# Expert loop: the bias add one slot ahead on GpSimd, the slot's first-layer weights by a DMA, and the relus first on VectorE

## The reference

```
logits = xf @ Wg.T
idx = jnp.argmax(logits, axis=-1)
out = jnp.zeros_like(xf)
for e in range(E):                      # E = 8, D = 128, DF = 512
    m = (idx == e)[:, None].astype(xf.dtype)
    h = jax.nn.relu(xf @ W1[e] + b1[e])
    out = out + m * (h @ W2[e] + b2[e])
...
z = _layer_norm(y + _moe(y, Wg, W1, b1, W2, b2), g2, be2)
```

## Time and profile before

| what | us |
|---|---|
| median of 3 runs | 1211.57 (1209.97 to 1211.81) |
| the profiled execution | 1201.12 |
| its span in the trace | 1199.3 |
| GpSimd busy in the span | 824.3 (69%) |
| VectorE busy | 923.1 (77%) |
| TensorE matmuls busy | 943.2 (79%) |
| ScalarE busy | 592.9 (49%) |
| the expert loop, from 972 to the end | 227 |

### The profile page before, as it was taken

One profiled execution on the slowest core, in us unless ns is written; L12 is line 12 of the kernel. 1 busy time (PEld: TensorE's weight loads), 2 busy tenths in 40 slices (PEclk: granted clock), 3 DMA queues, 4 the chain that ended last, 5 costly groups with the idle time before them and its releaser, 6 DMA issues. The chain is left out here.

```text
span 1199.3 us, 25297 instructions
## 1 busy us (share of the span) xinstructions
PE 943.2 (79%) x5489; PEld 681.6 (57%) x5489; DVE 923.1 (77%) x2728; ACT 592.9 (49%) x1554; POOL 824.3 (69%) x728
## 2 busy tenths in 40 slices
PE   3799999999688688889888816888768578777774
PEld 3465555555366355555555514566567577666663
DVE  3599999999769588888889845766655957777775
ACT  1655545554299466776666525666265013333331
POOL 0388888888422299999999946788144047888885
PEclk9899999999889799999999956999755559999998
DMA  7410000000000400000000051334322022233330
GB/s 213 134 52 1 0 0 0 0 0 1 1 1 1 140 10 9 17 17 9 17 17 18 10 157 40 95 98 105 92 84 79 1 68 83 88 91 91 90 89 24
DMA packets 67117, 61.25 MB, mean 51 GB/s; under 512 B 7812, under 2 KB 54096, under 8 KB 67042
## 3 DMA queue, kind: packets, MB, share of 16 engines
q1 hardware_dynamic: 58978, 41.47, 12.4%
q0 software_dynamic: 6912, 18.36, 5.3%
q10 hardware_dynamic: 1152, 0.52, 0.2%
HBM read 30.97 MB, written 21.50 MB: 44 GB/s over the span
## 5 line engine op out<-in xcount | busy, mean ns | idle before, releaser
L462 PE MATMUL a_pS<-a_kv,utri 128*128 128x360 f32 (+3 forms) x768 | 264.8, 481 | 19.3 <-issue 6.5
L453 POOL TENSOR_TENSOR a_kv<-a_qk,a_vv 128x1152 f32<-128x1152 f32 (+1 forms) x128 | 264.0, 2063 | 13.2 <-DVE a_qk L427 13.2
L558 POOL TENSOR_TENSOR a_tt<-a_tt 128x576 f32<-128x576 f32 (+1 forms) x128 | 156.9, 1226 | 64.4 <-DVE a_tt L542 64.3
L462 PEld LDWEIGHTS a_pS<-a_kv,utri 128*128 128x128 f32 x768 | 136.3, 191 | 100.4 <-DVE a_tt L542 30.5
L542 DVE TENSOR_TENSOR a_tt<-a_pS,a_qk 128x360 f32<-128x360 f32 (+3 forms) x384 | 180.9, 526 | 15.4 <-PE a_pS L462 8.5
L1759 POOL DMA_INDIRECT x_yl<-ys,e_row x72 | 70.1, 974 | 69.5 <-POOLq L1472 54.2
L570 DVE TENSOR_REDUCE a_nd<-a_tt 128x144 f32<-128x720 f32 (+3 forms) x128 | 104.3, 815 | 0.0
L508 ACT ACTIVATE a_tt<-a_pI 128x144 f32<-128x144 f32 (+1 forms) x96 | 40.0, 417 | 111.7 <-PE a_pI L470 111.6
L1765 POOL DMA_INDIRECT out_dram<-x_o,e_row_z x72 | 73.3, 1017 | 25.2 <-DVE x_o L1753 20.8
L1687 ACT ACTIVATE x_hT<-x_pA,x_w 128x128 f32<-128x128 f32 x144 | 45.0, 363 | 89.8 <-PE x_pB L1679 81.9
L501 PEld LDWEIGHTS a_pO<-wgate,a_yT 128*128 128x128 f32 x256 | 42.8, 194 | 81.0 <-issue 50.8
(11 more groups left out here) (260 smaller groups left out, 2437.6 us busy)
## 6 DMA issues: line engine op xcount, KB each, us to landing
ys<-gw SPq DMA_DIRECT2D x16, 256.0 KB, 3.7
xs<-X SPq DMA_DIRECT2D x16, 256.0 KB, 2.3
X<-xs SPq DMA_DIRECT2D x16, 256.0 KB, 5.5
m_kx<-m_kc SPq DMA_DIRECT2D x64, 64.0 KB, 2.0
ys<-X SPq DMA_DIRECT2D x16, 256.0 KB, 3.1
m_ax<-m_pc SPq DMA_DIRECT2D x64, 64.0 KB, 2.0
ys<-U SPq DMA_DIRECT2D x16, 256.0 KB
w<-in_L_ffn_W_dram SPq DMA_DIRECT2D x1, 2048.0 KB
```

The costliest lines, as they stand in the source:

```text
L453: pool.tensor_tensor(kv[:, t % 2, :, :, :], kk.unsqueeze(2).to_broadcast([P, H, J, D]), vv[:, t, :, :].unsqueeze(3).to_broadcast([P, H, J, ...
L462: pe.matmul(pS[c][:, 0:(h1 - h0) * SC], K.utri[:, :], flat[:, h0 * SC:h1 * SC], start=True, stop=True).then_inc(u_done, 1)
L558: pool.tensor_tensor(tt[:, t % 2, :, :, D // 2:D], tt[:, t % 2, :, :, D // 2:D], tt[:, t % 2, :, :, 0:D // 2], ALU.add).then_inc(half_done, 1)
```

## The change

- VectorE no longer copies `w1`. SP's queue issues a DMA of the same 644 numbers by 128 partitions (322 KB) from `K.w1` to the ring instead, SBUF to SBUF, with the expert's number read into a register on SP. It waits for the same buffer to be free (slot j-4's relus and bias add). Four semaphores, one for each buffer, tell TensorE and GpSimd that the weights are there.
- GpSimd adds the bias of slot j+1 in slot j, so one slot earlier against its gathers and scatters.
- VectorE's slot begins with `vec_h(j+1)`; `vec_mv` comes behind it.

```
+        w1_in = [sem(f"w1_in{s}") for s in range(4)]
...
-        def vec_w1(v, j):
-            e = load_expert(v, j)
-            wait(v, h_act, j - 3)
-            wait(v, yb_ready, j - 3)
-            v.tensor_copy(w1[:, j % 4, :], K.w1[:, ds(e, 1), :].rearrange("p a f -> p (a f)")).then_inc(w1_ready, 1)
+        def sp_w1(sp, j):
+            e = load_expert(sp, j)
+            wait(sp, h_act, j - 3)
+            wait(sp, h_vec, j - 3)
+            wait(sp, yb_ready, j - 3)
+            sp.dma_start(w1[:, j % 4, :], K.w1[:, ds(e, 1), :].rearrange("p a f -> p (a f)")).then_inc(w1_in[j % 4], 16)
+
+        def w1_arrived(e, j):
+            e.wait_ge(w1_in[j % 4], 16 * (j // 4 + 1))
...
-            pool.wait_ge(w1_ready, j + 1)
+            w1_arrived(pool, j)
...
-            pe.wait_ge(w1_ready, j + 1)
+            w1_arrived(pe, j)
...
-                sp.wait_ge(b1_in, 16)
+                sp.wait_ge(b1_ready, 1)
+                for j in range(SLOTS):
+                    sp_w1(sp, j)
+                for s in range(4):
+                    sp.wait_ge(w1_in[s], 16 * (SLOTS // 4))
...
+                pool_yb(pool, 0)
                 for j in range(SLOTS):
-                    pool_yb(pool, j)
+                    if j + 1 < SLOTS:
+                        pool_yb(pool, j + 1)
                     if j + AHEAD < SLOTS:
...
-                v.wait_ge(b1_ready, 1)
-                vec_w1(v, 0)
-                vec_w1(v, 1)
                 vec_h(v, 0)
                 for j in range(SLOTS):
-                    if j + 2 < SLOTS:
-                        vec_w1(v, j + 2)
+                    if j + 1 < SLOTS:
+                        vec_h(v, j + 1)
                     if j >= 4 and j % 4 == 0:
                         vec_mv(v, j // 4 - 1)
-                    if j + 1 < SLOTS:
-                        vec_h(v, j + 1)
                     vec_u(v, j)
```

More of the change, by code:

```diff
@@ L1634, in run_experts @@
         y_in, z_out = [sem(f"y_in{s}") for s in range(ROWS)], [sem(f"z_out{s}") for s in range(4)]
-        y_T, yT_ready, w1_ready, h_ps, h_act, h_vec, z_ps = (
-            sem(n) for n in ("y_T", "yT_ready", "w1_ready", "h_ps", "h_act", "h_vec", "z_ps"))
+        y_T, yT_ready, h_ps, h_act, h_vec, z_ps = (
+            sem(n) for n in ("y_T", "yT_ready", "h_ps", "h_act", "h_vec", "z_ps"))
+        w1_in = [sem(f"w1_in{s}") for s in range(4)]
         yb_ready, u_ready, bn_ready, mv_ready, sd_ready, rs_ready, tm_ready, o_ready = (
```

## The result

The changed kernel took 1219.94 us (median of 6 runs, 1214.3 to 1223.67), the kernel before 1211.53 us (6 runs, 1209.97 to 1215.0). The ratio is 1.0074, with a 95% interval of 1.0050 to 1.0098: slower, where I had forecast 1203.9 us and faster, and outside the range of 1199.5 to 1211.5.

The account below looks back on a forecast made before the run. GpSimd's closed ring of gather, scatter and bias add was taken to set the steady pace. Head +0.4, steady slots -3.7 and end -4.4 sum to -7.7 us: 1211.57 to 1203.9 us, 8-in-10 range 1199.5 to 1211.5.

Parts of the forecast that it names:

- The base: Whole kernel: sum against the profiled 1201.12 us, then carry the 10.45 us difference to the median of 1211.57.
- if GpSimd waits for `vec_o` in the steady part: Expert loop's steady part: sign of a wrong prediction, GpSimd waiting for VectorE's `vec_o`; no size given.
- The other two: Signs of a wrong prediction: gathers and scatters grow with the traffic, or TensorE waits for the DMA; no size given.
- Steady slots: 59 steady loop slots: GpSimd's instructions shorten beside idle neighbours, 2.962 to 2.90 us a slot, -3.7 us.
- My first rival: Gains eaten: GpSimd's instructions follow DMA traffic and stay at 2.96, head pays 3, end gives 3.4; 1211.2 us, chance 0.14.
- The end: Last gather to last scatter: GpSimd, one slot ahead, no longer waits; 19.2 instead of 23.59 us, -4.4.
- The head: Loop's start: first weights land later (+0.7), VectorE without copies gives -0.3; net +0.4 us, from -0.5 to +3.
- The DMA: Each slot's weight transfer: 1.14 us at 290 GB/s, DMA share 0.70, latency hidden in the steady part.
- the rival in which the DMA engines become the bound: Steady slots: SBUF transfers far below 290 GB/s, deciding at 165; at 120 GB/s 1248 us; chance 0.06 (DMA-bound).
- GpSimd is slowed by the DMA: Steady slots: DMA traffic adds 0.2 us a slot to gather and scatter together, +11.8; total 1219.4 us, chance 0.07.
- The copy locks GpSimd out: Steady slots: VectorE's 0.50 us copy is GpSimd's loss in every slot, -29.5 us; total 1178 us, chance 0.03.
- my sentence that the trace agrees with it: Claimed the trace fits the copy lock-out rule only where copy (0.85 us) and bias add (0.61) collide, not in the steady ring.

Follow-up runs that it names:

- after_again: The changed kernel, untouched, timed again on chip 4 against the kernel before: 1189.23 us, ratio 0.9964.
- before_again: The kernel before, unchanged, run on chip 3 for a second trace: 1194.9 us (one run).
- order_only: The kernel before, copies kept, with the changed order of GpSimd and VectorE and no weight DMA, on chip 2: 1217.13 us, ratio 1.0003.
- ghost_small: The kernel before plus an SP DMA of 32 KB a slot into a tensor nobody reads, on chip 3: ratio 0.9988, later 0.9979.
- lockstep: The changed kernel, TensorE's first layer of slot j also waiting for `vec_u` of slot j-2: ratios 0.9993 (chip 3), 0.9996 (chip 4), 1.0165 (chip 5).
- order_only_4: The kernel before, copies kept, with the changed order of GpSimd and VectorE and no weight DMA, on chip 3: 1203.68 us, ratio 1.0072.
- few_mm: The changed kernel with three of the second layer's four matmuls left out in each slot, on chip 3: 1188.41 us (one run).

## Why the prediction was wrong, step by step

**The base.** This is the step that failed. I summed against one execution of 1201.12 us and wrote "carry the difference to the median of 1211.57, which lies 10.45 higher", as if that distance were a constant outside the change. The trace behind the sum has no stall: none of its 146 signals between 1000 and 1150 us is late, and its steady part takes 174.75 us, like chip 3's. The executions that were timed were of another sort. The 1201.12 us are not among the six timed ones, of which the lowest took 1209.97, and the record doesn't say on which chip they were taken. They would be ordinary on chip 3, where the kernel before ran from 1190.9 to 1203.8 us; on chips 1, 2 and 5 none of its 33 timed executions came below 1209.97, and every trace that is known to be from there has stalls. So the trace was likely taken on a chip of the other kind. That chip 1 had one execution without a stall is not excluded.

What the runs showed in place of that step: on chip 1 GpSimd did not set the pace of the changed kernel. Its steady part grew by 23.2 us where I had -3.7, since gathers waited 29.4 us for `vec_o`, and VectorE in turn for TensorE's signals; "if GpSimd waits for `vec_o` in the steady part" was one of the signs of being wrong that I had named. The other two did not come: gathers and scatters did not grow, and in the steady part TensorE's waits were not for the DMA. That the timed executions of the kernel before held stalls as well, fewer of them, is likely and not shown, because no trace of it with stalls exists. Why signals come late stays open.

**What the change does without stalls** (after_again on chip 4 against before_again on chip 3, and against what I had written):

| part | predicted, us | before | after | measured, us |
|---|---|---|---|---|
| head, first gather to first waiting one | +0.4 | 20.82 | 20.50 | -0.3 |
| steady, 59 slots | -3.7 | 174.75 | 173.84 | -0.9 |
| last gather to last scatter | -4.4 | 23.60 | 19.11 | -4.5 |
| sum | -7.7 | | | -5.7 |

The timed medians of chip 4 differ by 5.24 us. So direction and places were right there, and one term was mis-sized. *Steady slots:* I took 1.00 for the scatter and 0.46 for the bias add, from rows where little else ran. They stayed at 1.021 and 0.494, with the copy gone. What the copy cost the ring was only its collisions, 505 to 494 ns. The neighbours do not matter in the way I assumed. My first rival had the number (instructions that "stay at 2.96"; measured 2.946) but not the reason: they do not follow the DMA traffic either, which doubled from a share of 0.30 to 0.61.

*The end* came out as worked: rows of after_again's timeline that answer to the earlier trace rows:

```profile
1163.78 0.97 POOL L1764 DMA_INDIRECT x_yl<-ys,e_row  x1 [0.16 <-issue]
...
1166.08 0.49 POOL L1674 TENSOR_TENSOR x_yb<-x_yl,x_w 128x128 f32<-128x128 f32 x1
...
1167.78 0.47 POOL L1674 TENSOR_TENSOR x_yb<-x_yl,x_w 128x128 f32<-128x128 f32 x1
...
1182.90 0.98 POOL L1770 DMA_INDIRECT out_dram<-x_o,e_row_z  x1 [0.30 <-issue]
```

2.30 to the first bias add (2.29 predicted), 1.70 a slot, 19.1 in all (19.2), and no wait over 0.33.

*The head:* in this trace the first weights came late, and it did not matter. SP issues at 971.98 and TensorE starts at 976.00, 4.0 us later where I took 3.0; in the eight other traces with this DMA it was 3.0 to 3.2 us, so the price was right:

```profile
971.98 7.41 SPq L1664 DMA_DIRECT2D x_w<-w  x5
...
976.04 1.20 PE L1684 MATMUL x_pA<-x_yT,x_w 128*128 128x128 f32 x4 [1.56 <-DMA x_w<-w]
```

From first gather to first layer pass 6.6 us here and 5.5 in the first trace of the changed kernel, against 4.7 in the trace of before (+0.8 at the usual price, where I had +0.7). A TensorE and a VectorE without copies caught up by the first gather that waits.

*The DMA* was cheaper than estimated. The line of after_again's queues for 1000 to 1180 us and its issues:

```profile
q1 hardware_dynamic: 8489, 19.44, 29.0%
...
x_w<-w SPq DMA_DIRECT2D x58, 322.0 KB, 2.5
```

29.0% of 180 us for 19.44 MB, which is 59 transfers, is 0.89 us of all 16 engines each, not 1.14, and the DMA share is 0.61, not 0.70; landing takes 2.5 us. So the weights went at 329.7 KB / 0.89 us = 370 GB/s, and the rival in which the DMA engines become the bound, deciding at 165, did not arise. (The 290 GB/s of the earlier trace rows came in packets of 2.0 KB, 0.87 MB in 438, and not from rows of 512 bytes, as I wrote.) Gathers land later, 3.6 us against 3.1, which nobody waits for.

**What the change does with stalls.** The changed kernel's trace on chip 1 has 251.1 us from first gather to the end, on chip 4 220.5: 30.6 us of stalls. The kernel before on chip 1 has a median of 1211.5, which is 1.8 more than its span. If its loop starts at 967 us, like that of the changed kernel's trace (966.7), 242.7 us are left for the loop, 16.5 above its stall-free 226.2. So the change would add 14 us of stall and save 5.7, which comes to the +8.4 us that was timed. That is an estimate, and the fit hangs on the start that I chose: over all traces the loop starts between 964.5 and 974.7 us, so the stalls of before could be 9 to 19 us, and the sum +6 to +16. That the change gains on chip 4 (-0.36%) and loses on chip 5 (+0.82%) agrees with such a split.

**The rivals.** *GpSimd is slowed by the DMA* named 1219.4, and 1219.9 was measured. That was luck: gather and scatter are 970 and 1022 ns, unchanged, and what it priced at +0.2 a slot isn't there. The loss has the size and another place, TensorE's signals. The Trainium skill, "SBUF — State Buffer", section "Who interferes with whom", says that a DMA never contends with a compute engine. For the durations of instructions these traces agree, at a DMA share of 0.61 as at 0.30. It does not follow that a DMA beside the engines is free for the kernel: one that nobody reads costs 1.01% on chip 2 and 0.35% on chip 4. *The copy locks GpSimd out* was worth nothing here, as argued: without any copy the scatter takes 1021 ns, with it 1020. The rule of the Trainium skill, "SBUF — State Buffer", section "SBUF: two separate sides", is not refuted by that, and my sentence that the trace agrees with it only in the earlier trace rows was wrong, as the earlier trace rows is a bias add and no DMA. Whether the copy lengthens an indirect DMA hangs on how the two meet. The gathers of order_only with a copy begun just ahead of them take 1.23 instead of 0.97 us, which agrees with the rule, and so does one scatter of before, 1.18 us at 998.29 with a copy from 998.97; the steady scatters, with a copy begun 0.1 us behind their start, take 1.02 us and the copy its 0.50, which does not. The copy does meet the bias add, at 0.62 instead of 0.49 us.

**What stays open.** Why TensorE's signals come late on some chips (2, 5 and the one called 1) and never on chips 3 and 4, or whether the chip is the cause at all: only chip 3 was timed twice, alike both times; why they do so in this loop only, and not in the 960 us ahead of it; and whether on such chips it is the DMA's bytes or their number that adds to it (ghost_small never met one). Shown is what the late signals do not need: the weights' DMA as such (order_only has them without it), TensorE running ahead, or its full load. Nor do DMAs stop: the packets of the weights' queue take as long in both kinds (a median of 0.104 us on chips 1 and 4), those of GpSimd's queue 0.132 us on chip 1 and 0.121 on chips 4 and 5.

## What to carry to other kernels

Where the profiled execution lies outside the timed ones, and further from their median than the effect that is forecast (here 10.45 us against 7.7), the trace is not of the execution that is timed: price the unknown part as a cost that the change can enlarge, and widen the range by it. Before a cause is taken from an experiment, time the changed kernel beside it on the same chip; "lockstep mends it" was the chip's doing, and on a chip with stalls lockstep doubled the loss. And of two edits that belong together one alone can be worse than none: the new order needs the copy gone (+0.72% without, on a chip without stalls), and there it was the end of the loop, not its steady ring, that paid.

## What the runs showed of the hardware

Chips differ by more than this change is worth, for one and the same program: 1194.5, 1195.6 and 1196.2 us against 1211.5, 1216.3 and 1216.6, with no median between; single executions ran up to 1203.8 us on the one kind and down to 1210.0 on the other. In the traces the expert loop takes 220 to 234 us on one kind and 248 to 265 on the other; the first trace of before, of an unnamed chip, has 226. Its start moves between 964 and 975 us from run to run. The loop's difference comes with signals of TensorE that reach waiting engines 0.5 to 6 us after its recorded work, while GpSimd and the DMA engines go on. The change is worth -0.36% on one kind (one chip) and +0.74 to +0.82% on the other. A 128x644 float32 copy of VectorE begun 0.1 us ahead of GpSimd's gather lengthens it from 0.97 to 1.23 us (order_only); begun 0.1 us behind the start of a scatter it changes neither (before); over a bias add it makes 0.62 of 0.49 us and takes 0.97 instead of 0.50 itself (order_only_4). TensorE's clock can stand at 0.83 through the loop (few_mm on chip 3) with no time lost.
